# The first expert stage's early half is routed and sent inside the last batch of attention

## What is computed

```
x = x + attention(layernorm(x))     # 16 heads of width 8, norm of q and k, causal softmax, output weights
x = x + ffn(layernorm(x))           # the mixture of experts, below
x = x + message(layernorm(x))       # 16 channels: sigmoid of a rank-64 product, used from both sides
x = x + ffn(layernorm(x))           # the same weights again

def ffn(y):
    h = y + layernorm1(y) @ attn_w.T
    t = layernorm2(h)
    logits = t @ gate_w.T                      # 8 experts
    the two best experts of each token, softmax of their two logits -> r
    return h + sum over both of r * down[e](silu(gate[e](t)) * up[e](t))
```

## Time and profile before

| what | us |
|---|---|
| median of three runs | 2870.96 |
| the profiled execution's own time | 2869.91 |
| its span | 2868.2 |
| last batch, group 1 to group 2 (603.5 to 639.1) | 35.6 |
| group 2 to group 3 (639.1 to 673.1) | 34.0 |
| group 3 to the last output copy (673.1 to 693.3) | 20.2 |
| output of the last group, end of attention (693.3 to 702.4) | 9.1 |
| first expert stage up to the late head (702.4 to 735.45) | 33.05 |
| late head, routing, first block's products (735.45 to 782.9) | 47.45 |

### The profile page before, as it was taken

The page is one execution under the profiler, slowest core; times in us unless marked ns, Lnnn a source line. Parts: engine busy times, 40 slices in busy tenths (PEclk is TensorE's granted clock), DMA queues, the critical chain, the costliest instruction groups (busy, mean ns, idle before and its releaser), DMA issues. The chain is left out here.

```text
span 2868.2 us, 53413 instructions
## 1 busy us (share of the span) xinstructions
PE 2675.3 (93%) x18798; PEld 1683.4 (59%) x18798; DVE 1756.0 (61%) x3424; ACT 1604.6 (56%) x2677; POOL 808.9 (28%) x1177
## 2 busy tenths in 40 slices
PE   5999998998599889999999999999999999995997
PEld 3555565665488745555555555555555555553886
DVE  7777777775666655555655555555556655555666
ACT  2666666666644455555555556565565555555443
POOL 4142422322456311111111111122121132220652
PEclk8999999999699999999999999999999999998998
DMA  6500000001344268888878887777777788885222
GB/s 108 81 16 16 8 16 16 16 16 52 96 122 147 72 166 193 188 188 194 193 186 188 188 188 185 183 183 178 182 186 184 179 193 200 199 197 199 68 87 86
DMA packets 196571, 383.17 MB, mean 134 GB/s; under 512 B 45281, under 2 KB 108906, under 8 KB 194954
## 3 DMA queue, kind: packets, MB, share of 16 engines
q1 hardware_dynamic: 187722, 362.55, 53.0%
q0 software_dynamic: 8640, 17.84, 1.9%
HBM read 38.10 MB, written 39.86 MB: 27 GB/s over the span
## 5 line engine op out<-in xcount | busy, mean ns | idle before, releaser
L2766 DVE STREAM_TRANSPOSE m_turned<-m_sig 128x1024 f32<-128x1024 f32 x512 | 613.8, 1228 | 480.7 <-ACT m_sig L2536 469.2
L2536 ACT ACTIVATE m_sig<-m_f_ps 128x1024 f32<-128x1024 f32 x512 | 496.5, 1022 | 283.5 <-PE m_f_ps L2368 283.2
L2381 PE MATMUL m_v_ps<-m_sig,m_tok 128*64 128x512 f32 x2048 | 497.4, 607 | 0.0
L2393 PE MATMUL m_v_ps<-m_sigT,m_tok 128*64 128x256 f32 x4064 | 461.1, 380 | 1.4 <-DMA m_sigT<-m_turned 1.4
L1042 DVE TENSOR_REDUCE a_maxima<-a_bank 128x1 f32<-128x512 f32 (+4 forms) x624 | 366.8, 643 | 123.4 <-PE a_bank L637 74.0
L801 ACT ACTIVATE a_prob<-a_bank 128x512 f32<-128x512 f32 (+1 forms) x608 | 321.5, 585 | 191.6 <-PE a_bank L649 188.4
L2368 PE MATMUL m_f_ps<-m_swap,m_own 64*128 64x512 f32 x1536 | 416.4, 404 | 8.0 <-DMA m_swap<-m_own 4.6
L2368 PE MATMUL m_f_ps<-m_own,m_swap 64*128 64x512 f32 x1536 | 416.6, 404 | 0.0
L2393 PEld LDWEIGHTS m_v_ps<-m_sigT,m_tok 128*64 128x64 f32 x4064 | 290.3, 137 | 198.3 <-issue 62.4
L2632 POOL TENSOR_TENSOR m_own<-m_uv,m_own 128x1024 fp32r<-128x1024 f32 x64 | 152.0, 2375 | 731.9 <-ACT m_own L2515 731.9
L2368 PEld LDWEIGHTS m_f_ps<-m_swap,m_own 64*128 64x128 f32 x1536 | 270.1, 186 | 102.3 <-issue 46.9
(11 more groups left out here) (464 smaller groups left out, 4373.0 us busy)
## 6 DMA issues: line engine op xcount, KB each, us to landing
m_sigT<-m_turned SPq DMA_DIRECT2D x2042, 128.0 KB, 2.3
m_swap<-m_own SPq DMA_DIRECT2D x64, 256.0 KB, 3.3
f_t_rows<-f_sent_rows SPq DMA_DIRECT2D x142, 65.0 KB, 2.1
f_sent_rows<-clear_rows SPq DMA_DIRECT2D x34, 260.0 KB, 9.2
k_apart<-a_kT SPq DMA_DIRECT2D x64, 128.0 KB, 2.4
m_swap<-m_own SPq DMA_DIRECT2D x64, 128.0 KB, 3.1
f_h<-back_rows SPq DMA_DIRECT2D x8, 512.0 KB, 5.1
rows<-back_rows SPq DMA_DIRECT2D x6, 512.0 KB, 4.2
```

The source lines that it names most:

```text
L2381: mm = pe.matmul(v2_ps[h * RANK:(h + 1) * RANK, :], tok[p][:, 0, j + s * SIDE, :], sig[j % 2][s][:, h * HALF:(h + 1) * HALF], start=(j == ...
L2393: mm = pe.matmul(v1_ps[h * RANK:(h + 1) * RANK, g * 2 * P:(g + 1) * 2 * P], tok[p][:, 1, jj, :], sigT[g][:, :, 2 * h:2 * h + 2, jj, :].rea ...
L2536: act.activation(sig[j % 2][s][:, :], f_ps[s][:, :], ACT.Sigmoid).then_inc(sig_ready, 1)
L2766: dve.transpose(turned[g][:, :, q, :, :], sig[j % 2][s][:, :].rearrange("p (t j a) -> p j t a", j=4, a=STACK)).then_inc(turn_ready, 1)
```

## The change

The early half of the first expert stage moves into groups 1, 2 and 3 of attention's last batch. `moe_phase` loses its `first_half` argument: both expert stages now start with the late half. In `f1` the early head, `choose`, count, places, table, plain rows, kept rows and the 32 sends are gone from all lists, and SyncE's loads of the factors no longer wait for the early table. The half moments and scales of the early half move from the last group's end to group 1. `a_proj` takes over the memory of `clear_rows`, so the first output projection of batch 0 waits for the clearing stores; squares, next values and the new early rows share one buffer.

```diff
+        STEPS = ((0, 3), (3, 6), (6, 9), (9, 12), (12, 14), (14, 16))
+        def early_steps(g, i):                       # after score unit i of group g
+            if g == 1:
+                yield from {0: [("half_moments", 0)], 2: [("half_dev", 0)], 3: [("half_scales", 0)]}.get(i, ())
+                if i in (4, 8, 12, 16):
+                    yield "plain_rows", i // 4 - 1
+                for n in range(len(STEPS)):
+                    at = 5 * n + 5
+                    if i in (at, at + 2, at + 5):
+                        yield {at: "head_rows", at + 2: "head_turn", at + 5: "head_product"}[i], n
+            elif g == 2:
+                if i in (1, 4, 7, 10):
+                    yield "add_rows", i // 3
+                yield from {0: [("second_moments", 0)], 2: [("second_dev", 0)], 3: [("second_scales", 0)], 5: [("route_first", 0)],
+                            8: [("route_second", 0)], 10: [("count", 0)], 12: [("route_blocks", 0)], 15: [("route_firsts", 0)],
+                            18: [("route_places", 0)], 21: [("early_table", 0)]}.get(i, ())
+                if 4 <= i < 4 + 2 * EARLY // 2 and i % 2 == 0:
+                    yield "keep_rows", i // 2 - 2
+            elif SCORE_UNITS - EARLY_SENDS <= i:     # 38 - 32 = 6
+                yield "send", i - (SCORE_UNITS - EARLY_SENDS)
...
+                if prev and not prep:                # at the end of each score unit's step
+                    yield from early_steps(g, i)
...
+            def head_turn(u, i):                     # TensorE: one unit
+                pe.wait_ge(head_normed, i + 1)
+                return turn_tiles(u, lambda t: head_norm[...], range(*STEPS[i]))
+            def head_product(u, i, turned):          # TensorE: one unit, 2 or 3 matmuls 128x144
+            def count(u):                            # TensorE: one unit, 3 matmuls 128x128
+                pe.wait_ge(chosen_ready, 1)
...
+            def head_rows(i):                        # ScalarE: 2 or 3 norm rows
+            def head_turned_rows(u, i):              # ScalarE: empties the turn's bank
+            def keep_rows(i):                        # ScalarE: 2 tiles
+                act.wait_ge(early_summed, i // 2 + 1)
+                act.wait_ge(second_scaled, 1)
...
+            def plain_rows(g):                       # GpSimd: two tensor_tensor 128x512
+            def add_rows(g):                         # GpSimd: x += own rows, 128x512
+            def send(j):                             # GpSimd
+                t, choice = divmod(j, TOP)
+                pool.wait_ge(places_ready, 1)
+                pool.wait_ge(rows_kept, t // 2 + 1)
+                pool.indirect_dma_start(k["sent_rows", "f1"][:, :], ..., early[:, t, :], None).then_inc(k["sent", "f1"][0], 16)
...
             for g in (1, 2, 3):
                 group(u, b, g, True, False, g < GROUPS - 1)
+            pool.wait_ge(k["sent", "f1"][0], 16 * EARLY_SENDS)
...
+            def head_sums(u, i):                     # VectorE: add, copy of the logits, 2 or 3 bn_stats
...
-            if not first_half:
-                head(0)
...
-                count(0)
...
-                keep_rows(0)
...
-                plain_half()
-                pool.wait_ge(places_ready, 1)
-                pool.wait_ge(norm_kept, HALF_GROUPS)
-                for j in range(SENT):
-                    send(0, j)
...
-                head(0)
-                choose(0)
-                late_sums()
-                dve.wait_ge(counts_full, 1)
-                upto = blocks_of(0, scan(0))
-                placed(0, upto)
-                rows_placed(0)
-                late_moments()
-                carry(upto)
-                early_table()
+            dve.tensor_copy(rows[1][:, :, DIM], k["sent_to"][:, tiles(1)])
+            late_sums()
+            late_moments()
```

More of the change, by code:

```diff
@@ L936, in group @@
                         stack_queries(b + 1 if g in (2, 3) else b, n)
+                    elif what == "plain_rows":
+                        plain_rows(n)
+                    elif what == "add_rows":
+                        add_rows(n)
+                    elif what == "send":
+                        send(n)
                 return projects
@@ L1090, in keep_turned, with half_sums @@
                 dve.tensor_copy(dst, src[:, :]).then_inc(u.free(), 1)
-            def group(u, link, b, g, prev, prep, follows):
+            def half_sums(link):
+                dve.wait_ge(v_ready, BATCH)
+                for e in range(EXPERTS):
+                    dve.memset(rank[:, e:e + 1], float(EXPERTS - e))
+                link(dve.tensor_copy(early[:, :, DIM], k["sent_to"][:, 0:EARLY]))
+                dve.wait_ge(half_stats, 1)
+                half_moments(dve, link, k, 0).then_inc(half_var, 1)
@@ new lines, in route_second, with take_counts @@
+            def route_second(link):
+                pick_first(link, other, second[:, 0:EARLY], first_at)
+                dve.tensor_tensor(chosen, pick, other, ALU.add).then_inc(chosen_ready, 1)
+            def take_counts(u):
+                src = u.next()
+                u.wait_full(dve)
+                for i, to in enumerate((earlier_rows, tile_counts)):
+                    dve.tensor_copy(to, src[:, i * ROUTE:(i + 1) * ROUTE].rearrange("p (t e) -> p t e", e=EXPERTS))
+                dve.tensor_copy(k["numbers"][:, :], src[:, 2 * ROUTE:2 * ROUTE + NB]).then_inc(u.free(), 1)
+                u.wait_emptied(dve, u.n)
@@ L1094, in group @@
+            def group(u, link, b, g, prev, prep, follows, head_made=()):
                 ahead, projected, queried = (g + 1) % GROUPS, [], False
@@ L1188, in moe_phase @@
     AHEAD, TURNS = 2, 3
-    GROUPS_BEFORE = first_half * HALF_GROUPS
+    GROUPS_BEFORE = HALF_GROUPS
     SUM_COLS = ALL * DIM // (2 * GROUPS_ALL)
@@ L1450, in count @@
             def count(a):
-                if not a:
-                    pe.matmul(tally[a][:, 2 * FLAT:2 * FLAT + P], k["ones"][:, :], k["below"][:, :], start=True, stop=True)
-                pe.wait_ge(chosen_ready, a + 1 - first_half)
+                pe.wait_ge(chosen_ready, 1)
                 flat = chosen[:, tiles(a), :].rearrange("p t e -> p (t e)")
```

343 lines of the change are left out of this document (253 added, 90 removed).

## The result

The changed kernel takes 2902.97 us (median of 4, 2901.63 to 2905.73) against 2870.55 (2869.77 to 2872.42) for the kernel before: ratio 1.0113, 95% interval 1.0096 to 1.0131. The forecast was 2900. The profiled execution took 2904.12 us, its span 2902.3, which is 34.1 more than before.

A forecast was written before the change was run, and what follows sets the result against it. Attention was taken as bound by TensorE, VectorE second, and the expert stage's first 33.05 us by no engine. 2869.91 + 22.5 + 25 + 1.5 - 19.8 = 2899.1, with the median's 1.05 forecast as 2900 us, full range 2884 to 2917.

The forecast's parts named there:

- Saved in the expert stage: Start of the expert stage: late head starts at 715.7 instead of 735.45, saving 19.8 us, bounds 17 and 22.
- at its present pace: Expert stage: the late head, once started, was let run as long as today, 47.45 us.
- Group 3: Attention's last group: selects wait behind 31 sends of 1.27 us on GpSimd, cost 25 us, bounds 24 and 26.5.
- The tail: Output work after the last select: TensorE's clock may be lower after its idle group, cost 1.5 us, bounds 0 and 4.2.
- Group 1's head: Among group 1's maxima: TensorE's 16 turns and 16 products cost 7.5 us, VectorE's 6.9 fit beside them.
- group 1's moments: Before group 1's maxima: 19 small VectorE operations, 3.6 us of work, taken to cost 3 us.
- group 2: Group 2: moments, logits and choices make it late by 5 us, places, table and counts' copies cost 7.
- Groups 1 and 2: Both groups together: 3 + 7.5 + 5 + 7 = 22.5 us, from 7.5 (TensorE's own work) to 34.
- One sign: Group 2: VectorE nearly full there was named as something that would show the forecast right.
- Rival 1: Group 3: sends hold GpSimd's queue for little, so group and tail cost nothing; 2874 or 2866 us, chance 0.05.
- Rival 2: Groups 1 and 2: VectorE's work falls into its idle time, they cost only TensorE's 7.5; 2885 us, chance 0.12.
- Rival 3: Long VectorE runs stall the six banks and TensorE's work comes on top, 34 in the sum; 2917 us, chance 0.12.

The follow-up runs named there:

- sends_in_f1: Changed kernel, but the 32 sends leave attention's last group for the start of GpSimd's list in the first expert stage; ratio 1.0045 to the kernel before.
- route_g3: As sends_in_f1, but all of group 2's added work (second moments, routing, count, table, additions, kept rows) stands in group 3; ratio 1.0018 to the kernel before.
- count_later: As sends_in_f1, but TensorE's count and all that follows it stand five units later in group 2; ratio 1.0039 to the kernel before.
- best1: As route_g3, but kept rows in the expert stage, count two units later, group 1's moments behind the query copies; ratio 1.0025 to the kernel before.
- adds_later: As sends_in_f1, but GpSimd's four additions in group 2 stand behind later score units, kept rows 10 units later; ratio 1.0049 to the kernel before.
- before_there: The kernel before, unchanged, traced on a variants' chip; first block's products 108.3 us after the expert stage's start, against 80.6 on the first chip.

## Why the prediction was right

- **Saved in the expert stage: 19.8 forecast, 19.95 measured** on the late head's start. The late head itself took 1.5 longer than "at its present pace", with a clock of 0.69 instead of 0.72; no run separates a cause.
- **Group 3: 25 forecast, 23.3 measured** (44.2 from select to select instead of 20.95). sends_in_f1 shows that it is the sends alone. The 1.7 of error is in the pair: I gave a send 1.27 and a select behind it 0.93. In the rows a send before a select is followed at once by it: 739.26 to 741.20 is 1.94 for both, and the 0.30 of issue isn't there. Seven pairs at 0.26 less are 1.8. The rule of the Trainium skill ("DMA: Bandwidth & Descriptors", "Anatomy of one DMA") that descriptor generation is small doesn't hold for these sends of 128 rows: the trace has 0.96 us of queue for each.
- **The tail: 1.5 forecast, 0.8 measured**, clock 0.78. The reason given, the idle time of TensorE in group 3, isn't borne out: sends_in_f1 has group 3 as before and a tail of 9.95 at 0.83, and route_g3 one of 9.0 at 1.00. What lowers the clock there stays open.
- **Group 1's head: 7.5 forecast for turns and products, 7.0 measured** (B of route_g3, where group 2 has no routing). That TensorE's own instructions are the price, and VectorE's fit beside them, is right.
- **Too small: group 1's moments (3, measured 5.9) and group 2 (12, measured 4.7 + 11.2 = 15.9)**, together 6.8. Both terms counted how late TensorE would be, and left out that its clock falls behind a stall: 3.0 us of wait in group 1 became 5.9. In C TensorE's work takes 40.19 us instead of 33.33, with four more matmuls and a clock of 0.85, so of the 11.3 us some 7 are slower work and 4.4 idle time. That the clock sets C's length isn't shown: with 0.89 in count_later C is as long, and TensorE waits longer for VectorE. Groups 1 and 2 were forecast at 22.5 and took 28.9 (5.9 + 11.7 + 11.3), still inside the bounds of 7.5 and 34.
- **One sign was wrong**: VectorE isn't nearly full in group 2. It has 35.25 of 45.27, and TensorE has 40.19, a part of it at the lower clock. Its busy time doesn't set the length by itself; what counts is who waits for it in that place: best1 moved VectorE's routing to where few wait for it.
- **The total is closer than its terms, and that part is luck.** Errors of opposite sign: -1.7, -0.7 and -0.2 in the three terms above, +6.4 in groups 1 and 2, +1.5 in the late head, -0.6 outside all of them. That is +4.7 on the sum of 2899.1, and the profiled execution has 2904.12. The median is 1.15 below that execution, where the forecast had put it 1.05 above; so 5.0 too little in the sum became 3.0 in the forecast.

Rival 1 fell with group 3: the sends hold the queue 1.26 us each, and TensorE waits 18.9 us for the selects. Rival 2 (2885) fell with B and C of 47.3 and 45.3 and TensorE's waits in them. Rival 3 (2917) had the mechanism that showed, stalled banks, but priced it as all of VectorE's work in a row.

## What to carry to other kernels

Before work is moved beside a bound engine, read who waits for whom in the new place: the same routing cost 16.0 us in a group where TensorE is busy 33 of 34 us and VectorE 25, and 9.9 in one where VectorE is idle, or 3.5 with ScalarE's part taken out and the count later. A stall put into TensorE's busy stretch is to be counted with the slower clock behind it: 3.0 us of waits went with 5.9 in group 1, and 5.9 with 11.3 in C. A send on GpSimd is 0.96 us of its queue and 1.26 in a row; nine fitted into idle time for 0.1 us and 31 in front of selects cost 23.

## What the hardware showed unexpectedly

**VectorE stands still for GpSimd, for whole instructions.** Group 2, VectorE's choices, and then GpSimd's additions of the same moments:

```profile
653.50 0.29 DVE L1312 SCALAR_TENSOR_TENSOR a_spare<-a_zT,a_spare 128x128 f32<-128x128 f32 x1
...
654.14 0.29 DVE L1304 TENSOR_TENSOR a_zT<-a_spare,second 128x128 f32<-128x128 f32 x1
654.47 1.15 DVE L1305 TENSOR_TENSOR a_zT<-a_zT,a_spare 128x128 f32<-128x128 f32 x1
655.66 0.29 DVE L1306 TENSOR_REDUCE a_spare<-a_zT 128x16 f32<-128x128 f32 x1
655.98 0.83 DVE L1307 TENSOR_TENSOR a_zT<-a_zT,a_spare 128x128 f32<-128x128 f32 x1
```

```profile
654.25 2.40 POOL L1053 TENSOR_TENSOR x<-x,a_spare 128x512 f32<-128x512 f32 x2
```

The multiplication at 654.47 takes 1.15 instead of 0.29 and ends 0.17 after the first addition (655.45, half of GpSimd's 2.40); the one at 655.98 ends at 656.81, 0.16 after the second (656.65). The reduction between them has one input and runs beside GpSimd in its usual 0.29. This is the exclusive lock on the shared pair of ports of the Trainium skill ("SBUF — State Buffer", "Who interferes with whom"), with two-input operations of VectorE as its victims; the trace agrees. It is a part of group 2's cost; how large a part isn't measured, since adds_later only moved the collision from B (1.4 shorter) to C (2.1 longer).

**Chips differ in what sends do to other engines.** On all four other chips the kernel before takes 63 to 68 us longer than on the first, and before_there has it in three stretches in which indirect DMAs run: F (27.7), the blocks up to the message stage (236.9 instead of 219.1) and all behind the message stage (334.7 instead of 313.0). Attention's stretches A to E and the message stage agree within 0.5 us. But the message stage has 32 sends of its own, three per channel, at 0.96 us each as well, and isn't longer. So sends alone don't do it; what must come with them is open. That the chip makes the difference is inferred from one that has it not and four that have it.
